# A GRU scan beside a mixture of experts: two halves of the first expert layer, and VectorE's order inside a step

## The chip, the cores and the metric

One core of one Trainium2 chip. The metric is the device time of one launch in microseconds (us), the median of several executions. Lower is better.

## What is computed

A fused model of two blocks over x of 8 batches, 256 time steps and 256 features: two recurrences with attention and expert layers, added to x in turn. The change lies in the last addition alone, a gated recurrent scan whose output feeds a mixture of eight experts and one shared expert:

```python
def step(h, xs):
    xzt, xrt, xht = xs
    z = jax.nn.sigmoid(xzt + h @ U_z + vz)
    r = jax.nn.sigmoid(xrt + h @ U_r + vr)
    hh = jnp.tanh(xht + r * h @ U + vh)
    h_new = (1.0 - z) * h + z * hh
    return (h_new, h_new)
...
gate = jnp.einsum('bsd,ed->bse', x, Wg) + routing_bias
_, top_idx = jax.lax.top_k(gate, K)
probs = jax.nn.softmax(masked_gate, axis=-1)
out = _swiglu(x, Ws1, Ws2, Ws3)
h1 = jnp.einsum('bsd,ehd->ebsh', x, W1)
h2 = jnp.einsum('bsd,ehd->ebsh', x, W2)
eo = jnp.einsum('ebsh,edh->ebsd', jax.nn.sigmoid(h1) * h1 * h2, W3)
out = out + jnp.einsum('ebsd,bse->bsd', eo, weights)
```

## The kernel before

The last stage is `pipeline_two`. It cuts the 256 time steps into 16 chunks of 16 steps (C = 16, with 8 batches a step, so CW = 128 columns a chunk). Every engine runs the same list `steps()`, pairs (i, slot): i is the chunk in the scan, slot the step in it. There is no planner: the order of calls in each engine's loop is the order of the work, and semaphores tie the loops together. A wait on an engine holds all that stands behind it on that engine.

Two kinds of work run interleaved. **The scan** of chunk i is a chain from step to step. TensorE adds U times the state for two gates (`zr_gates`, 24 small matmuls, lines L1754 and L1760; the first 16 wait for the high half of the state, the last 8 for its low half). ScalarE takes a tanh (`zr`, L1871). VectorE makes the product of gate and state in high and low halves (`reset_product`: rh_h L2030, rh L2032, rh_l L2036) and a part of the new state (zc, L2063). TensorE does the candidate (12 small matmuls, L1771 and L1776), ScalarE its tanh (`cand`, L1876), and VectorE the new state (`new_state`: zm L2042, g_hh L2047, h L2049, g_hl L2053), which the next step's `zr_gates` waits for.

**The experts** work on chunk i - 1. The hidden units of all nine experts are cut into 48 tiles, three to a group, 16 groups to a chunk, one group a slot. For group n: `hidden` on TensorE (36 matmuls of 128x128, L103: 18 for the first matrix of the layer into bank p1, 18 for the second into p2), `half_tanh` on ScalarE (th, L1895) from p1, and one slot later `swiglu` on VectorE (uu L1942 from th and p1, then a L1951 from uu and p2), `high` on ScalarE (a_h, L1886) and the low half on GpSimd (a_l, L1928). Two slots later comes `down` on TensorE (9 matmuls of 128x256, L1812). In nine of the 16 slots (0, 2, 4, 6, 7, 9, 11, 12 and 14) an expert is complete and `add_expert` adds it on VectorE (acc, L1967).

Some slots hold more, under `misc`: slot 0 reads the routing logits (lg, L1976) and, in `swiglu`, multiplies by the experts' weights (uw, L1947); slots 1 and 2 do the routing on VectorE (max, subtraction L1981, index, cast L1985; then L1988, L1991, L1994 and three more up to wts, L2000); slot 2 adds the input products of half a chunk on TensorE; slot 3 writes the output; slot 6 takes in the next chunk on VectorE (hs L1679, gx_h L2014, gx_l L2016); slot 8 splits the routing weights (wt_h on ScalarE L1914, wt_l on VectorE L2020); slot 12 adds the input products of the other half.

The order of one step on each engine is, before the change:

```python
# TensorE: zr_gates, misc, hidden, candidate, down
# ScalarE: reset_gates, high, candidate, half_tanh
# VectorE: swiglu, add_expert, reset_product, zc, misc, new_state
```

Of the kernel before, what the change touches and what calls it, by code (L numbers as in the profile page):

```python
# [26 lines left out]
ALU = mybir.AluOpType  # L27
# [9 lines left out]
CW = C * B  # L37
# [1414 lines left out]
GM = 3  # L1452
# [23 lines left out]
def pipeline_two(nc, t, arena, attd, x2d, m12_h, m12_l, out):  # L1476

    with ExitStack() as ctx:
# [3 lines left out]
        def sem(name):  # L1482
            return ctx.enter_context(nc.semaphore(name))
# [94 lines left out]
        def tile(name, dt=F16):  # L1578
# [34 lines left out]
        zr_pe, zr_act, u_pe, u_act = (sem(n) for n in ("zr_pe", "zr_act", "u_pe", "u_act"))  # L1613
        rh_hi, rh_32, rh_lo, z_parts, z_mix, h_new, h_hi, h_lo = (
            sem(n) for n in ("rh_hi", "rh_32", "rh_lo", "z_parts", "z_mix", "h_new", "h_hi3", "h_lo3"))
        hid_pe, th_act, u_done, uw_done, a_done, a_hi, a_lo, w3_pe, po_free = (
            sem(n) for n in ("hid_pe", "th_act", "u_done", "uw_done", "a_done", "a_hi3", "a_lo3", "w3_pe", "po_free"))
        z_full, z_free = sem("z_full3"), sem("z_free3")
        route, exp_done, wt_hi, wb_done = (sem(n) for n in ("route3", "exp3", "wt_hi3", "wb_done"))
        x3_done, x3_split, out_done = (sem(n) for n in ("x3_done", "x3_split", "out_done"))  # L1620
# [119 lines left out]
        def _(pe):  # L1740
# [36 lines left out]
                                         start=False, stop=(k == KT - 1), skip_group_check=True)  # L1777
                last.then_inc(u_pe, 1)

            def hidden(i, slot):  # L1780
                n = group(i, slot, 0)
                if n is None:
                    return
                par = (i - 1) % 2
                if slot == 0:
                    pe.wait_ge(h_lo, i * C)
                if n >= 2:
                    pe.wait_ge(a_done, n - 1)
                for mat, bank in enumerate((p1[n % 2], p2[n % 2])):
                    for j in range(GM):  # L1790
                        w = (lambda k: m12_h[:, mat, k, GM * slot + j, :], lambda k: m12_l[:, mat, k, GM * slot + j, :])
                        last = split_matmul(pe, bank[:, j * CW:(j + 1) * CW], w,
                                            (lambda k: g_hh[:, par, k, :], lambda k: g_hl[:, par, k, :]), j == 0,
                                            last=True)
                last.then_inc(hid_pe, 1)

            def down(i, slot):
                n = group(i, slot, 2)
# [48 lines left out]
            for i, slot in steps():  # L1847
                if scans(i):
                    zr_gates(i, slot)
                    if slot == 2:  # L1850
                        if i > 0:
                            pe.wait_ge(u_act, i * C)
                        project_half(pe, 1)
                    if slot == 12 and scans(i + 1):
                        pe.wait_ge(x3_split, 2 * (i + 1))
                        pe.wait_ge(u_act, i * C + 8)
                        project_half(pe, 0)
                misc(i, slot)
                hidden(i, slot)
                if scans(i):  # L1860
                    candidate(i, slot)
                if (i, slot) == (1, 2):
                    pe.wait_ge(m3_lo, NG)
                down(i, slot)


        @block.scalar
        def _(act):
            def reset_gates(i, slot):
                act.wait_ge(zr_pe, i * C + slot + 1)  # L1870
                act.activation(zr[:, :], g_b[slot // 8][:, slot % 8, 0:4].rearrange("p m b -> p (m b)"), ACT.Tanh,  # L1871
                               scale=0.5 / S).then_inc(zr_act, 1)

            def candidate(i, slot):
                act.wait_ge(u_pe, i * C + slot + 1)
                act.activation(cand[:, :], g_b[slot // 8][:, slot % 8, 4:6].rearrange("p m b -> p (m b)"), ACT.Tanh,  # L1876
                               scale=1.0 / S).then_inc(u_act, 1)

            def high(i, slot):
                n = group(i, slot, 1)  # L1880
                if n is None:
                    return
                act.wait_ge(a_done, n + 1)
                if n >= 2:
                    act.wait_ge(w3_pe, n - 1)
                act.activation(a_h[:, n % 2, :], a32[:, n % 2, :], ACT.Copy).then_inc(a_hi, 1)  # L1886

            def half_tanh(i, slot):
                n = group(i, slot, 0)
                if n is None:  # L1890
                    return
                act.wait_ge(hid_pe, n + 1)
                if n >= 2:
                    act.wait_ge(u_done, n - 1)
                act.activation(th[:, n % 2, :], p1[n % 2][:, 0:GM * CW], ACT.Tanh, scale=0.5 / S).then_inc(th_act, 1)  # L1895

            act.activation(cand[:, 0:1], wts[:, 0:1], ACT.Exp)
            for i, slot in steps():
                if scans(i):
                    reset_gates(i, slot)  # L1900
                high(i, slot)
                if i == 0:
                    act.wait_ge(m3_staged[slot % 4], 16 * (slot // 4 + 1))
                    staged, hi, _lo = piece(slot)
                    act.activation(hi, staged, ACT.Copy, scale=S).then_inc(m3_hi, 1)  # L1905
                if scans(i):
                    candidate(i, slot)
                half_tanh(i, slot)
                if slot == 1 and 1 <= i <= NCH:
                    act.wait_ge(route, NR * (i - 1) + 2)  # L1910
                    act.activation(rt[:, 1, :], rt[:, 0, :], ACT.Exp).then_inc(exp_done, 1)
                if slot == 8 and 1 <= i <= NCH:
                    act.wait_ge(z_full, Z3_AT[i, slot] + 1)
                    act.activation(wt_h[:, :], z[0:EA, 0:P], ACT.Copy, scale=S).then_inc(wt_hi, 1)  # L1914
                if slot == 10 and 1 <= i <= NCH:
                    act.wait_ge(z_full, Z3_AT[i, slot] + 1)
                    if i > 1:
                        act.wait_ge(uw_done, i - 1)
                    act.activation(wb[:, :], z[:, 0:GM * CW], ACT.Copy).then_inc(z_free, 1)
# [13 lines left out]
        def _(dve):  # L1933
            def swiglu(i, slot):
                n = group(i, slot, 1)
                if n is None:
                    return
                weighted = n % NG == REM
                dve.wait_ge(th_act, n + 1)
                if n >= 1:  # L1940
                    dve.wait_ge(a_done, n)
                dve.scalar_tensor_tensor(out=uu[:, :], in0=th[:, n % 2, :], scalar=1.0,  # L1942
                                         in1=p1[n % 2][:, 0:GM * CW], op0=ALU.add, op1=ALU.mult).then_inc(u_done, 1)
                dve.wait_ge(u_done, n + 1)
                if weighted:
                    dve.wait_ge(z_free, Z3_AT[n // NG + 1, 10] + 1)
                    dve.tensor_tensor(uw[:, :], uu[:, :], wb[:, :], ALU.mult).then_inc(uw_done, 1)  # L1947
                    dve.wait_ge(uw_done, n // NG + 1)
                if n >= 2:
                    dve.wait_ge(a_lo, n - 1)  # L1950
                dve.scalar_tensor_tensor(out=a32[:, n % 2, :], in0=(uw if weighted else uu)[:, :], scalar=0.5 / S / S,  # L1951
                                         in1=p2[n % 2][:, 0:GM * CW], op0=ALU.mult, op1=ALU.mult).then_inc(a_done, 1)

# [99 lines left out]
                dve.tensor_tensor(hl, h32[:, :].rearrange(kb, b=B), hh, ALU.subtract).then_inc(h_lo, 1)  # L2053

            for i, slot in steps():
                swiglu(i, slot)
                add_expert(i, slot)
                if scans(i):
                    reset_product(i, slot)
                if slot == 0:  # L2060
                    misc(i, slot)
                if scans(i):
                    dve.scalar_tensor_tensor(out=zc[:, :], in0=zr[:, 0:16], scalar=1.0, in1=h32[:, :],  # L2063
                                             op0=ALU.subtract, op1=ALU.mult).then_inc(z_parts, 1)
                if slot != 0:
                    misc(i, slot)
                if i == 0:
                    dve.wait_ge(m3_hi, slot + 1)
                    staged, hi, lo = piece(slot)
                    dve.scalar_tensor_tensor(out=lo, in0=staged, scalar=S, in1=hi, op0=ALU.mult,  # L2070
                                             op1=ALU.subtract).then_inc(m3_lo, 1)
                if scans(i):
                    new_state(i, slot)
# [86 lines left out]
```

## Time and profile before

| | us |
|---|---|
| median of 3 runs | 2818.0 |
| lowest and highest run | 2813.54 and 2818.51 |
| the profiled execution's own time | 2814.62 |
| its span | 2812.6 |
| TensorE busy, matmuls | 2424.7 |
| TensorE busy, weight loads | 2022.1 |
| VectorE busy | 1965.6 |
| ScalarE busy | 1144.6 |
| GpSimd busy | 431.1 |
| mean granted TensorE clock, share of full speed | 0.94 |

The page lists for each engine what it was busy with and what ended its idle time. The changed stage begins near 1680 us of the span and ends with it; its scan of chunks 1 to 15 runs from 1729 to 2688 us. Matmuls are pipelined, and an idle TensorE shows better in the start times of the weight loads than in the busy share of the matmuls.

### The profile page before, as it was taken

The page shows a single profiled execution, that of the slowest core. Times are in us where ns is not written, and L with a number is a line of the kernel's source. Part 1 is how long each engine was busy: PE and PEld are TensorE (multiplying, and loading weights), DVE is VectorE, ACT ScalarE, POOL GpSimd, SP SyncE. Part 2 cuts the span into 40 slices and gives each one's busy share as a digit, 9 for nine tenths or more (in the row PEclk, how much of TensorE's full clock was granted, in tenths as well). Part 3 has the DMA queues.
Part 4 walks back from the last instruction along what each step waited for, and adds up shares of the span by engine and source line. Part 5 has one row for each costly group of instructions (what it writes and reads, how often), then busy time and mean ns, then how long its engine had stood idle before and what let it go on. Part 6 is the DMA issues. An engine that isn't in the chain of part 4 may idle for free. (4 is left out here: it accounts for less than half of the span.)

```text
span 2812.6 us, 119114 instructions
## 1 busy us (share of the span) xinstructions
PE 2424.7 (86%) x50764; PEld 2022.1 (72%) x50764; DVE 1965.6 (70%) x7376; ACT 1144.6 (41%) x3659; POOL 431.1 (15%) x404
## 2 busy tenths in 40 slices
PE   1678999999999999987547846999999999999999
PEld 0455677777777777654216636999999999999998
DVE  4567777777777777787578736777766777777775
ACT  3124555555555555566126623333333333333333
POOL 0000000000000000000029910222222222222222
PEclk9778999999999999999669967999999999999999
DMA  5000000000000000000013332000000000000000
GB/s 166 2 2 2 5 5 5 5 5 5 5 5 5 5 5 5 5 5 4 3 69 87 88 90 57 9 9 9 11 9 9 9 9 9 9 9 9 5 5 6
DMA packets 52745, 53.77 MB, mean 19 GB/s; under 512 B 24678, under 2 KB 46839, under 8 KB 50041
## 3 DMA queue, kind: packets, MB, share of 16 engines
q1 hardware_dynamic: 47284, 27.79, 3.6%
q0 software_dynamic: 2000, 14.68, 1.5%
q8 instruction: 402, 6.59, 1.0%
q10 hardware_dynamic: 2934, 3.69, 0.4%
q14 instruction: 125, 1.02, 0.1%
HBM read 39.59 MB, written 6.55 MB: 16 GB/s over the span
## 5 line engine op out<-in xcount | busy, mean ns | idle before, releaser
L103 PE MATMUL p<-g_hl,m_h 128*128 128x128 f16 x3072 | 528.7, 219 | 0.0
L103 PE MATMUL p<-g_hh,m_h 128*128 128x128 f16 x3072 | 528.7, 219 | 0.0
L103 PE MATMUL p<-g_hh,m_l 128*128 128x128 f16 x3072 | 528.6, 219 | 0.0
L765 DVE STREAM_TRANSPOSE gt<-lg_b 128x512 f32<-128x512 f32 x324 | 230.3, 711 | 216.5 <-PE lg_b L448 202.6
L1928 POOL TENSOR_TENSOR a_l<-a,a_h 128x384 f16<-128x384 f32 x256 | 233.9, 914 | 915.9 <-ACT a_h L1886 915.9
L642 ACT ACTIVATE gl<-gt 128x128 f32<-128x128 f32 x324 | 100.2, 309 | 629.2 <-DVE gt L765 629.1
L657 ACT ACTIVATE hm<-xy,b 128x512 f32<-128x512 f32 x512 | 347.4, 678 | 0.1
L103 PEld LDWEIGHTS p<-g_hh,m_h 128*128 128x128 f16 x3072 | 300.4, 98 | 1.8
L103 PEld LDWEIGHTS p<-g_hh,m_l 128*128 128x128 f16 x3072 | 300.6, 98 | 0.7
L103 PEld LDWEIGHTS p<-g_hl,m_h 128*128 128x128 f16 x3072 | 300.7, 98 | 0.0
L448 PE MATMUL lg_b<-a_wh_hi,lh 128*32 128x256 f16 x4096 | 217.4, 291 | 79.0 <-DVE lh L789 76.8
L448 PE MATMUL lg_b<-e_wh_hi,lh 128*32 128x256 f16 x4096 | 209.6, 282 | 47.5 <-DVE lh L789 46.8
L448 PEld LDWEIGHTS lg_b<-a_wh_hi,lh 128*32 128x32 f16 x4096 | 100.6, 100 | 161.7 <-DVE lh L789 130.4
L1812 PE MATMUL po<-m_h,a_h 128*128 128x256 f16 x768 | 208.5, 271 | 1.9 <-DVE acc L1967 1.9
L1812 PE MATMUL po<-m_h,a_l 128*128 128x256 f16 x768 | 209.0, 272 | 0.0
L1812 PE MATMUL po<-m_l,a_h 128*128 128x256 f16 x768 | 208.8, 272 | 0.0
L1876 ACT ACTIVATE cand<-g_b 128x16 f32<-128x16 f32 x256 | 46.9, 183 | 382.8 <-PE g_b L1776 382.8
L614 PE MATMUL yo<-hm,w2f 128*32 128x256 f32 x2048 | 161.5, 388 | 34.8 <-DVE tmp L815 34.7
L2042 DVE SCALAR_TENSOR_TENSOR zm<-zr,cand 128x16 f32<-128x16 f32 x256 | 44.3, 173 | 201.2 <-ACT cand L1876 200.3
L1886 ACT ACTIVATE a_h<-a 128x384 f16<-128x384 f32 x256 | 133.9, 523 | 106.1 <-DVE a L1951 106.1
L1754 PEld LDWEIGHTS g_b<-g_hh,gu_w 128*128 128x128 f16 x4096 | 136.5, 96 | 50.9 <-DVE g_hh L2047 45.8
L1754 PE MATMUL g_b<-g_hh,gu_w 128*128 128x8 f16 x4096 | 140.5, 166 | 35.9 <-DVE g_hh L2047 34.8
(421 smaller groups left out, 6900.7 us busy)
## 6 DMA issues: line engine op xcount, KB each, us to landing
m_stage<-in_m_w POOLq DMA_DIRECT2D x12, 1024.0 KB, 5.3
hs<-in_m_w SPq DMA_DIRECT2D x16, 384.0 KB, 3.2
xs<-in_x POOLq DMA_DIRECT2D x1, 2048.0 KB, 8.4
x_dram<-x SPq DMA_DIRECT2D x16, 128.0 KB, 2.2
s_v<-in_l_wv SPq DMA_DIRECT2D x1, 2048.0 KB
attention_dram<-att SPq DMA_DIRECT2D x16, 128.0 KB, 2.7
attr<-attention_dram SPq DMA_DIRECT2D x128, 16.0 KB, 1.7
x2r<-x_dram SPq DMA_DIRECT2D x16, 128.0 KB, 2.5
```

The source lines that it names most:

```text
L103: ins = pe.matmul(out, w[wp](k), x[xp](k), start=start, stop=last and k == KT - 1 and xp == 1, skip_group_check=True)
L448: last = pe.matmul(gate_block(ae, j, par), lh[:, part, ae, k, u, :], columns(w[name], k, j), start=False, stop=(part == 1 and k == KT - 1) ...
L614: last = pe.matmul(yo[q * HD:(q + 1) * HD, :, :], w2f[:, n % E1, :], tok[:, :, q, :], start=True, stop=True, skip_group_check=True, tile_p ...
L642: act.activation(gl[:, :].rearrange("p (m b) -> p m b", b=B), gt[:, :].rearrange("p (m n) -> p m n", n=32)[:, :, slot % QS * B:(slot % QS ...
L657: act.activation(hm32[:, n % 2, h * 512:(h + 1) * 512], xy[h][:, :], ACT.Gelu, bias=b1[:, n % E1:n % E1 + 1], scale=1.0 / S).then_inc(g_32, 1)
L765: dve.transpose(gt[:, :], lg_b[slot // QS % 2][:, :, :, :].rearrange("p g a x -> p (g a x)"))\
L1754: pe.matmul(o[:, slot % 8, m, :], w[:, k, m * P:(m + 1) * P], h(g_hh, k), start=False, stop=False, skip_group_check=True)
L1812: last = pe.matmul(po[:, half, :], x[:, n % 2, r], w[:, tl, :], start=(first and x is a_h and w is m3_h), stop=(end and x is a_l), skip_gr ...
L1876: act.activation(cand[:, :], g_b[slot // 8][:, slot % 8, 4:6].rearrange("p m b -> p (m b)"), ACT.Tanh, scale=1.0 / S).then_inc(u_act, 1)
L1886: act.activation(a_h[:, n % 2, :], a32[:, n % 2, :], ACT.Copy).then_inc(a_hi, 1)
L1928: pool.tensor_tensor(a_l[:, n % 2, :], a32[:, n % 2, :], a_h[:, n % 2, :], ALU.subtract).then_inc(a_lo, 1)
L2042: dve.scalar_tensor_tensor(out=zm[:, :], in0=zr[:, 0:16], scalar=1.0, in1=cand[:, :], op0=ALU.add, op1=ALU.mult).then_inc(z_mix, 1)
```

## The change

The order in each step is now:

```python
# TensorE: zr_gates, misc, hidden (first matrix), candidate, hidden (second matrix), down
# ScalarE: reset_gates, half_tanh, candidate, high
# VectorE: reset_product, zc, misc of slot 0, swiglu, add_expert, misc, new_state
```

The first matrix's end is told by `hid_pe` as before, the second's by a new semaphore `gate_pe`, for which VectorE's last product `a` now waits as well. No operation is added or taken away.

```diff
-            def hidden(i, slot):
+            def hidden(i, slot, mat):
                 n = group(i, slot, 0)
...
-                if slot == 0:
+                if slot == 0 and mat == 0:
                     pe.wait_ge(h_lo, i * C)
-                if n >= 2:
+                if n >= 2 and mat == 0:
                     pe.wait_ge(a_done, n - 1)
-                for mat, bank in enumerate((p1[n % 2], p2[n % 2])):
-                    for j in range(GM):
...
+                bank = (p1, p2)[mat][n % 2]
+                for j in range(GM):
...
+                last.then_inc((hid_pe, gate_pe)[mat], 1)
...
                 misc(i, slot)
-                hidden(i, slot)
+                hidden(i, slot, 0)
                 if scans(i):
                     candidate(i, slot)
+                hidden(i, slot, 1)
...
-                high(i, slot)
+                half_tanh(i, slot)
                 if i == 0:
...
                 if scans(i):
                     candidate(i, slot)
-                half_tanh(i, slot)
+                high(i, slot)
...
                 if n >= 2:
                     dve.wait_ge(a_lo, n - 1)
+                dve.wait_ge(gate_pe, n + 1)
...
             for i, slot in steps():
+                if scans(i):
+                    reset_product(i, slot)
+                    dve.scalar_tensor_tensor(out=zc[:, :], in0=zr[:, 0:16], scalar=1.0, in1=h32[:, :],
+                                             op0=ALU.subtract, op1=ALU.mult).then_inc(z_parts, 1)
+                if slot == 0:
+                    misc(i, slot)
                 swiglu(i, slot)
                 add_expert(i, slot)
-                if scans(i):
-                    reset_product(i, slot)
-                if slot == 0:
-                    misc(i, slot)
-                if scans(i):
-                    dve.scalar_tensor_tensor(out=zc[:, :], in0=zr[:, 0:16], scalar=1.0, in1=h32[:, :],
-                                             op0=ALU.subtract, op1=ALU.mult).then_inc(z_parts, 1)
                 if slot != 0:
                     misc(i, slot)
```

Here is VectorE's order at slot 6 of a middle chunk, the slot that takes in the next chunk, before the change (line, operation, written tile, read tiles, shape, semaphores waited for):

```order
L1942 SCALAR_TENSOR_TENSOR uu<-th,p 128x384 [waits a_done,th_act]
L1951 SCALAR_TENSOR_TENSOR a<-uu,p 128x384 [waits a_lo3,u_done]
L1967 SCALAR_TENSOR_TENSOR acc<-po,wts,acc 128x256 [waits po_free,w3_pe]
L2030 SCALAR_TENSOR_TENSOR rh_h<-zr,h 128x16 [waits h_new,zr_act]
L2032 SCALAR_TENSOR_TENSOR rh<-zr,h 128x16
L2036 TENSOR_TENSOR rh_l<-rh,rh_h 128x16 [waits rh_32,rh_hi]
L2063 SCALAR_TENSOR_TENSOR zc<-zr,h 128x16
L1679 TENSOR_TENSOR hs<-z,x2r 128x2x128 [waits z_full3]
L2014 TENSOR_SCALAR gx_h<-hs 128x256 [waits x3_done]
L2016 TENSOR_TENSOR gx_l<-hs,gx_h 128x256 [waits x3_split]
L2042 SCALAR_TENSOR_TENSOR zm<-zr,cand 128x16 [waits u_act]
```

And the same slot in the changed kernel, whose line numbers are a little other:

```order
L2032 SCALAR_TENSOR_TENSOR rh_h<-zr,h 128x16 [waits h_new,zr_act]
L2034 SCALAR_TENSOR_TENSOR rh<-zr,h 128x16
L2038 TENSOR_TENSOR rh_l<-rh,rh_h 128x16 [waits rh_32,rh_hi]
L2060 SCALAR_TENSOR_TENSOR zc<-zr,h 128x16
L1943 SCALAR_TENSOR_TENSOR uu<-th,p 128x384 [waits a_done,th_act]
L1953 SCALAR_TENSOR_TENSOR a<-uu,p 128x384 [waits gate_pe,a_lo3,u_done]
L1969 SCALAR_TENSOR_TENSOR acc<-po,wts,acc 128x256 [waits po_free,w3_pe]
L1679 TENSOR_TENSOR hs<-z,x2r 128x2x128 [waits z_full3]
L2016 TENSOR_SCALAR gx_h<-hs 128x256 [waits x3_done]
L2018 TENSOR_TENSOR gx_l<-hs,gx_h 128x256 [waits x3_split]
L2044 SCALAR_TENSOR_TENSOR zm<-zr,cand 128x16 [waits u_act]
```

The three expert products have moved from ahead of the scan's product to between it and the new state, and hs, gx_h and gx_l now stand straight behind them.

ScalarE's order at slot 8, where the routing weights are split, before:

```order
L1871 ACTIVATE zr<-g_b 128x32 [waits zr_pe]
L1886 ACTIVATE a_h<-a 128x384 [waits w3_pe,a_done]
L1876 ACTIVATE cand<-g_b 128x16 [waits u_pe]
L1895 ACTIVATE th<-p 128x384 [waits u_done,hid_pe]
L1914 ACTIVATE wt_h<-z 9x128 [waits z_full3]
```

and in the changed kernel:

```order
L1872 ACTIVATE zr<-g_b 128x32 [waits zr_pe]
L1896 ACTIVATE th<-p 128x384 [waits u_done,hid_pe]
L1877 ACTIVATE cand<-g_b 128x16 [waits u_pe]
L1887 ACTIVATE a_h<-a 128x384 [waits w3_pe,a_done]
L1915 ACTIVATE wt_h<-z 9x128 [waits z_full3]
```

th and a_h have changed places around cand, and wt_h stands behind a_h instead of th.

## Rows read from the trace of the kernel before

**Rows 1.** Slots 0, 2, 5, 8, 9: length, busy PE, PEld, DVE, ACT, POOL, clock, DMA.

```profile
2003.20:2007.76 4.56, 4.40 (x91) 4.16 (x88) 3.93 (x13) 1.29 (x4) 0.91 (x1) 1.00 0.01 4
2011.66:2016.95 5.29, 5.29 (x132) 5.18 (x129) 4.22 (x17) 1.28 (x4) 0.91 (x1) 1.00 0.01 3
2025.07:2028.96 3.89, 3.89 (x84) 3.79 (x82) 2.08 (x10) 1.29 (x4) 0.91 (x1) 1.00 0.00 0
2037.45:2042.19 4.74, 4.28 (x85) 3.89 (x82) 2.23 (x11) 1.42 (x5) 0.91 (x1) 1.00 0.11 31
2042.19:2046.20 4.01, 3.95 (x80) 3.77 (x81) 3.25 (x12) 1.28 (x4) 0.91 (x1) 1.00 0.01 4
```

**Rows 2.** Timeline, two waits of the weight loads in chunk 5 (start us, us, engine).

```profile
2006.77 0.17 PEld L1776 LDWEIGHTS g_b<-rh_l,gu_w 128*128 128x128 f16 x4 [0.25 <-DVE rh_l L2036]
...
2033.22 0.18 DVE L2047 SCALAR_TENSOR_TENSOR g_hh<-zc,zm 128x16 f16<-128x16 f32 x1
...
2033.45 0.47 PEld L1754 LDWEIGHTS g_b<-g_hh,gu_w 128*128 128x128 f16 x16 [0.35 <-DVE g_hh L2047]
```

**Rows 3.** Timeline, weight loads of slot 5 of chunk 5.

```profile
2025.55 0.27 PEld L1760 LDWEIGHTS g_b<-g_hl,gu_w 128*128 128x128 f16 x8
2025.75 0.10 PEld L103 LDWEIGHTS p<-g_hh,m_h 128*128 128x128 f16 x1
...
2027.73 0.31 PEld L1771 LDWEIGHTS g_b<-rh_h,gu_w 128*128 128x128 f16 x8
```

**Rows 4.** Timeline, ScalarE, VectorE and GpSimd, end of slot 5 and slot 6.

```profile
2028.26 0.18 ACT L1876 ACTIVATE cand<-g_b 128x16 f32<-128x16 f32 x1 [1.30 <-PE g_b L1776]
...
2028.48 0.17 DVE L2042 SCALAR_TENSOR_TENSOR zm<-zr,cand 128x16 f32<-128x16 f32 x1 [1.53 <-ACT cand L1876]
2028.69 0.17 DVE L2047 SCALAR_TENSOR_TENSOR g_hh<-zc,zm 128x16 f16<-128x16 f32 x1
...
2029.06 0.17 DVE L2053 TENSOR_TENSOR g_hl<-h,g_hh 128x16 f16<-128x16 f32 x1
...
2029.75 0.55 DVE L1951 SCALAR_TENSOR_TENSOR a<-uu,p 128x384 f32<-128x384 f32 x1
...
2029.85 0.20 ACT L1871 ACTIVATE zr<-g_b 128x32 f32<-128x32 f32 x1 [1.02 <-PE g_b L1760]
...
2030.22 0.48 DVE L1967 SCALAR_TENSOR_TENSOR acc<-po,wts,acc 128x256 f32<-128x256 f32 x1
...
2030.94 0.92 POOL L1928 TENSOR_TENSOR a_l<-a,a_h 128x384 f16<-128x384 f32 x1 [2.98 <-ACT a_h L1886]
```

**Rows 5.** Timeline, VectorE beside GpSimd, attention stage and slot 4 of chunk 5.

```profile
1525.06 5.38 POOL L1211 TENSOR_SCALAR m_stage<-m_stage 128x2048 f32<-128x2048 f32 x1
1527.80 2.99 DVE L1376 TENSOR_SCALAR xn_h<-hs 128x512 f16<-128x512 f32 x1
...
2023.08 0.91 POOL L1928 TENSOR_TENSOR a_l<-a,a_h 128x384 f16<-128x384 f32 x1 [3.23 <-ACT a_h L1886]
2023.11 0.91 DVE L2036 TENSOR_TENSOR rh_l<-rh,rh_h 128x16 f16<-128x16 f32 x1
```

**Rows 6.** Groups by form, VectorE, last stage (count; busy us, mean ns).

```profile
L2016 DVE TENSOR_TENSOR gx_l<-hs,gx_h 128x256 f16<-128x256 f32 x14 | 6.0, 426 | 0.5
L1679 DVE TENSOR_TENSOR hs<-z,x2r 128x256 f32<-128x256 f32 x14 | 5.7, 410 | 0.0
...
L2014 DVE TENSOR_SCALAR gx_h<-hs 128x256 f16<-128x256 f32 x14 | 4.1, 294 | 0.5
```

**Rows 7.** Timeline, slot 8 and slot 2 of chunk 5.

```profile
2015.02 0.17 DVE L1994 TENSOR_TENSOR rt<-rt 128x8 f32<-128x8 f32 x1
...
2015.62 0.23 DVE L2000 TENSOR_SCALAR wts<-rt,sm 128x8 f32<-128x8 f32 x1
...
2041.22 0.25 ACT L1914 ACTIVATE wt_h<-z 9x128 f16<-9x128 f32 x1
...
2041.57 0.28 DVE L2020 SCALAR_TENSOR_TENSOR wt_l<-z,wt_h 9x128 f16<-9x128 f32 x1 [2.24 <-ACT wt_h L1914]
```

More of the change, by code:

```diff
@@ L1615, in pipeline_two @@
             sem(n) for n in ("rh_hi", "rh_32", "rh_lo", "z_parts", "z_mix", "h_new", "h_hi3", "h_lo3"))
-        hid_pe, th_act, u_done, uw_done, a_done, a_hi, a_lo, w3_pe, po_free = (
-            sem(n) for n in ("hid_pe", "th_act", "u_done", "uw_done", "a_done", "a_hi3", "a_lo3", "w3_pe", "po_free"))
+        hid_pe, gate_pe, th_act, u_done, uw_done, a_done, a_hi, a_lo, w3_pe, po_free = (
+            sem(n) for n in ("hid_pe", "gate_pe", "th_act", "u_done", "uw_done", "a_done", "a_hi3", "a_lo3", "w3_pe", "po_free"))
         z_full, z_free = sem("z_full3"), sem("z_free3")
@@ L1784, in hidden @@
                 par = (i - 1) % 2
-                if slot == 0:
+                if slot == 0 and mat == 0:
                     pe.wait_ge(h_lo, i * C)
-                if n >= 2:
+                if n >= 2 and mat == 0:
                     pe.wait_ge(a_done, n - 1)
-                for mat, bank in enumerate((p1[n % 2], p2[n % 2])):
-                    for j in range(GM):
[L1791 to L1795, printed above, removed]
+                bank = (p1, p2)[mat][n % 2]
+                for j in range(GM):
+                    w = (lambda k: m12_h[:, mat, k, GM * slot + j, :], lambda k: m12_l[:, mat, k, GM * slot + j, :])
+                    last = split_matmul(pe, bank[:, j * CW:(j + 1) * CW], w,
+                                        (lambda k: g_hh[:, par, k, :], lambda k: g_hl[:, par, k, :]), j == 0,
+                                        last=True)
+                last.then_inc((hid_pe, gate_pe)[mat], 1)
             def down(i, slot):
```

## Prediction

> **What bounds the kernel now.** I read the busy times by stretch first, then the timeline of single steps. From chunk 1 on TensorE is the bound: a step without extras lasts 3.89 us and TensorE is busy for all of it [rows 1]. In the times below 0 is the start of a step's first weight load. `zr_gates` takes to 0.68 (its low half starts at 0.48), the 36 matmuls of `hidden` to 2.66, so half of them is 0.99 [rows 3], and candidate and `down` fill the rest to 3.89. All other work lies beside this. TensorE loses time only where a state comes late: 0.25 us in slot 0 and 0.35 at the end of slot 6 [rows 2], most of what slot 8 is longer than a plain step (4.74 against 3.89), and 0.12 in slots 7 and 9 (4.01 [rows 1]). That is the pool from which a new order can win, some 2 us a chunk.
>
> **The change on TensorE.** Nothing is added; the candidate moves from 2.66 to 0.68 + 0.99 = 1.67. Can it be fed? ScalarE's zr tanh runs from 0.89 to 1.09 (2029.85 in a step that began at 2028.96 [rows 1, 4]). VectorE starts 0.04 after what it waits for (cand to zm [rows 4]), and the scan's product is now its first work: rh_h 1.13 to 1.30, and rh_l by the spacing of g_hh and g_hl (0.37, then 0.17 long [rows 4]) ends at 1.67. TensorE takes up a result 0.05 later (g_hh ended at 2033.40, its load began at 2033.45 [rows 2]), so 1.35 and 1.72 are possible and 1.67 and 1.90 are wanted: no wait. ScalarE's th now stands ahead of cand. th and a_h are 0.91 together (1.29 busy [rows 1] less zr's 0.20 and cand's 0.18 [rows 4]), so th ends some 0.5 after it may start at 1.9, and cand near 2.5. That costs nothing, since VectorE is busy longer, as follows.
>
> **The change on VectorE.** An operation that waits for nothing starts 0.08 ahead of the end of the one before (acc behind a [rows 4]); zc and uu follow rh_l so, and uu starts near 1.66. a ends at 2.81 (uu and a are alike, 0.55 each [rows 4], with 0.04 between). Where an expert is complete acc follows, 0.48 long [rows 4], to 3.21. The new state comes behind these. g_hh ends 0.38 after zm starts and g_hl starts 0.58 after it [rows 4]. In plain steps zm is at 2.73, g_hh ends at 3.11, and the next gates are wanted at 3.89: no wait, over 0.7 to spare. The third semaphore that a waits for I take at nothing, since acc of other steps waits for three at no visible gap; its upper end is 0.05 us.
>
> **What comes late next is the low half of the state.** In slot 4, rh_l starts 0.03 after GpSimd's a_l and then takes 0.91 us instead of 0.17, ending 0.03 behind it [rows 5]: the two do not run beside each other. a_l starts 0.64 after a's end (2030.30 to 2030.94 [rows 4]), nearly all of it a_h, and takes 0.91. In the new order that is 3.45 to 4.36. In plain steps g_hl starts at 3.31, ahead of a_l. With acc it is due at 3.71, inside a_l, so it ends at 4.39 and feeds TensorE at 4.44. The low gates are wanted at 3.89 + 0.48 = 4.37. That is 0.07 lost.
>
> The sum per chunk, by slot, as new length less old:
> - Slots 5, 10, 13, 15 (plain) and 3, 12 (extra TensorE work covers all): 0.
> - Slots 4, 11, 14 (acc): 0.07 lost now by g_hl, about as much before by rh_l in the same collision: 0. Slots 7 and 9: 3.96 against 4.01 [rows 1], -0.05 each.
> - Slot 1: max, subtraction and cast put g_hl behind a_l's start, +0.07.
> - Slot 0: lg, then uu, uw, a (0.55 each) and acc. g_hh ends near 4.30 and the gates start at 4.35 (4.31 is wanted: 4.56 [rows 1] less the 0.25 idle [rows 2]); a_l runs 4.23 to 5.14, TensorE has g_hl at 5.22 and wants it at 4.83. 4.35 + 0.39 = 4.74 against 4.56, +0.18.
> - Slot 2: L1994 reads two tiles like rh_l and is due, two short operations behind acc, at about 3.57, inside a_l; it ends at 4.39, and what follows it takes 0.66 more (2015.19 to 2015.85 [rows 7]). zm at 4.97, g_hh 0.38 later, gates at 5.40 against 5.29 [rows 1]: +0.11.
> - Slot 8: wt_h now waits for a_h, not for the candidate. a_h ends at 3.37, wt_h starts 0.10 ahead of that, 0.25 long, wt_l starts 0.10 later, 0.28 long [rows 7]: 3.90. zm 3.83, gates at 4.24 against 4.74 [rows 1]: -0.50. This is the gain of the change.
> - Slot 6: acc, hs (0.41), gx_h (0.29), gx_l (0.43) [rows 6] now stand behind the expert products and ahead of zm. hs reads PSUM and runs 3.13 to 3.54. gx_h is due at 3.57, inside a_l. What does it cost? From below its own 0.29. From above, it waits for a_l. In the attention stage the same kind of operation (a scale from f32 to f16) took 2.99 us beside a GpSimd operation that ended at 1530.44, itself ending at 1530.79 [rows 5], 0.35 after, on 512 columns where gx_h has 256; rh_l, with 16, ended 0.03 after. I take the upper end, with the middle of the two, 0.20, after a_l: gx_h ends 4.56, gx_l 5.03, zm 4.95, gates at 5.38. The slot took 2033.45 - 2028.96 = 4.49 [rows 1, 2]: +0.89.
>
> Ahead of the choice at slot 6: the rows show one blocked scale and one blocked subtraction, and they decide it. The Trainium skill (SBUF — State Buffer, the section on two separate sides) says that VectorE and GpSimd share a pair of ports under an exclusive lock, and that whichever starts first holds it for the whole instruction. By that rule gx_h, L1994 and g_hl all wait for a_l, as I have it; without the rule gx_h alone might pass. The same rule says that one SBUF input outside the two-port modes does not contend, so uu, a, acc, hs and the high halves pass, as the rows of this trace have them.
>
> Sum: 0.18 + 0.07 + 0.11 + 0.89 - 0.10 - 0.50 = +0.65 us a chunk, times 13 chunks (2 to 14) = +8.4. Chunk 1 has no uw and no acc at slots 0 and 2: +0.4. Chunk 15 has no slot 6 work: -0.2. Chunk 16 has no scan. At the very end the last group's th and uu start half a `hidden` earlier, and a, a_h, a_l, the last `down` and the output all follow it: -0.95. Total +7.6 us. Against the profiled execution (2814.62 us) that is 2822.2. The median of the runs, 2818.0, stands 3.4 above that execution; I set the forecast on the middle of the two, 2816.3, and come to 2824.
>
> **Rivals.**
> 1. gx_h passes beside a_l. Its rows of before never met a_l, and xn_h met other GpSimd operations. Then gx_h ends at 3.87, gx_l (two SBUF tiles) waits to 4.64, gates at 4.99: +0.50 at slot 6 instead of +0.89, times 14 is -5.5, total +2.1, about 2818. This is not slower by what can be measured. It decides from the point where a_l starts after gx_h's 3.57, or where a scale in two halves of width does not need GpSimd's port.
> 2. Nothing is blocked in the new order, as if a_l came second everywhere: slot 6 costs 0.20, slot 0 gains 0.21, the acc slots gain 0.08 each in three and 0.12 in two, slot 8 gains 0.50. That is near -1.0 a chunk, -15 in all, about 2801. Every row of a_l beside a two-tile subtraction speaks against it; a chain of mine that is 0.15 too late or too early would speak for it.
> 3. VectorE is later than I have it. At slot 1 the cast L1985 is due at 3.29 and a_l at 3.45. If 0.16 slips, the cast waits to 4.39 and the gates to 4.74: +0.8 in 15 chunks, +12 more. Or the third semaphore of a costs its 0.05 in nine slots: +6 more. 2830 to 2836.
> 4. The change does not do what it says: the printed order shows that it does, and I give it nothing.
>
> **How the numbers follow.** The forecast case 0.55, rival 1 0.17, rival 2 0.16, rival 3 0.12. A measurement of this kernel tells 0.2% from no change, here 5.6 us. The forecast of +7.6 is over that with 0.46 and under it with 0.09, since half its sum is slot 6. Slower: 0.46 + 0.12 = 0.58. Same: 0.09 + 0.17 = 0.26. Faster: 0.16. The range takes in rival 1 on the lowest run shown (2813) and the lower part of rival 3 (2833), and leaves out rival 2.
>
> **What would show it.** Right: plain steps at 3.89; cand running on TensorE between two blocks of 18; slot 6 near 5.4 with gx_h some 1 us long and ending behind a_l; slot 8 near 4.24; g_hl 0.7 us long in steps with acc; the wait ahead of slot 9 under 0.3. Wrong: gx_h at 0.29 beside a_l (rival 1), g_hl at 0.17 throughout (rival 2), L1985 near 1 us, or plain steps over 3.89 because the candidate waits for rh_h (rival 3 and worse).

## The result, and the profile after

| | before | after |
|---|---|---|
| median, us | 2815.77 (4 runs, 2812.98 to 2818.51) | 2864.06 (4 runs, 2857.84 to 2874.11) |
| the profiled execution's own time | 2814.62 | 2858.98 |
| its span | 2812.6 | 2857.1 |
| chunks 1 to 14 | 1728.94 to 2688.22: 959.3 | 1732.67 to 2729.89: 997.2 |
| chunk 5 | 68.44 | 71.15 |
| chunk 15, up to the start of its last step | 62.7 | 65.5 |
| from there to the end | 61.7 | 61.8 |

The changed kernel takes 1.0155 times the time before, with a 95% interval of 1.0121 to 1.0189: slower, where slower was forecast, but by 48 us and not by 7.6. The time of 2864.06 lies outside the range of 2813 to 2833. Of the 44.5 us between the two spans, 37.9 lie in chunks 1 to 14, 2.8 in chunk 15, 0.1 behind it and 3.7 ahead of chunk 1. (The stretch from 1729 to 2688 us of the kernel before, called the scan of chunks 1 to 15 above, ends where chunk 15 begins: it holds 14 chunks. The chunks are counted from 0, and the first one has no expert work.) Here are the first two rows of the page of the changed kernel (busy time, share, instructions).

```profile
span 2857.1 us, 119117 instructions
...
PE 2442.1 (85%) x50764; PEld 2020.1 (71%) x50764; DVE 1965.5 (69%) x7376; ACT 1138.2 (40%) x3659; POOL 429.9 (15%) x404
```

The work is the same: the weight loads take 2020.1 us where they took 2022.1, and VectorE is busy for 1965.5 against 1965.6. The time is idle time. The windows of chunk 5 show the steps in which it lies. First slots 0 to 3, 5, 6, 8, 9 and 11, then the whole chunk, in the columns of [rows 1].

```profile
2017.38:2022.38 5.00, 4.40 (x91) 4.11 (x89) 3.54 (x13) 1.28 (x4) 1.23 (x2) 1.00 0.01 3
2022.38:2026.80 4.42, 4.16 (x84) 3.79 (x81) 3.23 (x15) 1.38 (x5) 1.05 (x2) 1.00 0.01 4
2026.80:2032.07 5.27, 5.26 (x129) 5.11 (x130) 4.11 (x18) 1.17 (x4) 0.91 (x1) 1.00 0.01 3
2032.07:2036.43 4.36, 4.35 (x85) 3.98 (x84) 3.20 (x12) 1.29 (x4) 0.91 (x1) 1.00 0.01 3
...
2040.55:2044.44 3.89, 3.89 (x84) 3.79 (x82) 2.22 (x11) 1.28 (x4) 0.59 (x2) 1.00 0.00 0
2044.44:2049.74 5.30, 4.48 (x86) 4.05 (x84) 3.94 (x13) 1.28 (x4) 1.36 (x2) 1.00 0.04 9
...
2053.85:2058.49 4.64, 4.28 (x85) 3.89 (x83) 2.70 (x11) 1.44 (x5) 1.05 (x2) 1.00 0.01 1
2058.49:2062.60 4.11, 3.96 (x80) 3.72 (x81) 3.02 (x13) 1.28 (x4) 0.78 (x1) 1.00 0.02 4
```

```profile
2067.02:2071.23 4.21, 4.05 (x84) 3.81 (x82) 2.83 (x12) 1.28 (x4) 0.78 (x1) 1.00 0.00 0
2017.37:2088.52 71.15, 68.32 (x1412) 64.49 (x1410) 48.24 (x187) 20.85 (x67) 14.60 (x17) 1.00 0.03 8
```

The whole chunk, slot by slot:

| slot | before | forecast | after |
|---|---|---|---|
| 0 | 4.56 | 4.74 | 5.00 |
| 1 | 3.90 | 3.97 | 4.42 |
| 2 | 5.29 | 5.40 | 5.27 |
| 3 | 4.15 | 4.15 | 4.36 |
| 4 | 3.97 | 3.97 | 4.12 |
| 5 | 3.89 | 3.89 | 3.89 |
| 6 | 4.49 | 5.38 | 5.30 |
| 7 and 9, each | 4.01 | 3.96 | 4.11 |
| 8 | 4.74 | 4.24 | 4.64 |
| 11 and 14, each | 3.97 | 3.97 | 4.21 |

Slots 10, 12, 13 and 15 moved by 0.01 at most. Slot 10 lasts 4.42 in both kernels, so it is no plain step, though the forecast lists it as one; its term of 0 was right all the same. Two things are to be seen. The plain step and slots 6 and 2 came out near the forecast. And the rest splits into steps with an acc (0, 4, 7, 9, 11, 14), each 0.15 to 0.26 over the forecast, and three others, 1, 3 and 8, each 0.21 to 0.45 over it.

**The acc steps.** The chain of waits gives a first hint: it stands at 11% on VectorE and 25% on TensorE, where it stood at 7% and 30% before. The table of TensorE's waits from 1850 to 2650 us names the place (us in total, times, longest). Before, the same table held only g_hh, 5.6 us, and rh_l, 2.0 us.

```profile
PE g_b L1754 <- DVE g_hh L2049: 17.1, 35, 0.8
PE po L1812 <- DVE acc L1969: 13.5, 56, 0.6
PE po L1812 <- DVE acc L1967: 1.7, 11, 0.2
```

A new wait: `down` (L1812) for acc. In the timeline of slot 7, which begins at 2049.74:

```profile
2051.89 0.55 DVE L1953 SCALAR_TENSOR_TENSOR a<-uu,p 128x384 f32<-128x384 f32 x1
2052.36 0.48 DVE L1969 SCALAR_TENSOR_TENSOR acc<-po,wts,acc 128x256 f32<-128x256 f32 x1
2052.95 0.10 PEld L1812 LDWEIGHTS po<-m_h,a_h 128*128 128x128 f16 x1 [0.30 <-issue]
2052.98 0.27 PE L1812 MATMUL po<-m_h,a_h 128*128 128x256 f16 x1 [0.15 <-DVE acc L1969]
```

acc adds po into the sum, and `down` of the next group writes po. TensorE waits in front of it for `po_free`, that is until every expert that an earlier group completed has been added. acc follows a, ends at 3.10 of the step, and the load of `down` starts 0.11 behind that, with 0.30 us idle ahead of it. Before, VectorE did acc early, in slot 6 for one from 1.26 to 1.74 of the step [rows 4], and the table had no wait of `down`.

The wait asks for more than the buffer needs. By the code po has two halves, which the experts use in turn (`half = (n // NG * EA + e) % 2`), and in all nine acc slots `down` writes the half that acc does not read: in slot 7 acc reads expert 2 and `down` writes expert 3, whose half was free once expert 1 had been added in slot 6. `po_free` is a count, and `down` waits for it to include the expert just completed. A kernel in which this wait is one lower was not run, so what it would give is not shown.

**The other three.** Slots 3 and 8 in the timeline, and then the ranges of the two operations over the whole run (count; min, median, max ns; first and last start):

```profile
2035.43 0.91 POOL L1929 TENSOR_TENSOR a_l<-a,a_h 128x384 f16<-128x384 f32 x1 [3.45 <-ACT a_h L1887]
2035.49 0.89 DVE L2049 SCALAR_TENSOR_TENSOR g_hh<-zc,zm 128x16 f16<-128x16 f32 x1
...
2057.28 0.91 POOL L1929 TENSOR_TENSOR a_l<-a,a_h 128x384 f16<-128x384 f32 x1 [3.30 <-ACT a_h L1887]
2057.46 0.28 DVE L2022 SCALAR_TENSOR_TENSOR wt_l<-z,wt_h 9x128 f16<-9x128 f32 x1 [0.82 <-ACT wt_h L1915]
2057.67 0.55 DVE L2044 SCALAR_TENSOR_TENSOR zm<-zr,cand 128x16 f32<-128x16 f32 x1
```

```profile
L2049 DVE SCALAR_TENSOR_TENSOR g_hh<-zc,zm x256: 174/175/889, 1682.0 to 2798.3; 128x16 f16<-128x16 f32 x128
...
L2044 DVE SCALAR_TENSOR_TENSOR zm<-zr,cand x256: 161/168/556, 1681.8 to 2798.1; 128x16 f32<-128x16 f32 x128
```

g_hh and zm, 0.17 us long otherwise, are stretched until a_l is done: g_hh starts 0.06 after a_l and ends at 2036.38, 0.04 behind a_l's end at 2036.34. The forecast had taken only subtractions and the scale as held and had let "the high halves pass". Both operations read two tiles in SBUF, as the held subtractions do. In slot 8 wt_l, of whose two inputs z lies in PSUM, begins inside a_l and takes its usual 0.28.

The trace of before had a row of this kind, which the rows above lack; zc reads zr and h, both in SBUF:

```profile
2078.17 0.91 POOL L1928 TENSOR_TENSOR a_l<-a,a_h 128x384 f16<-128x384 f32 x1 [3.05 <-ACT a_h L1886]
2078.20 0.92 DVE L2063 SCALAR_TENSOR_TENSOR zc<-zr,h 128x16 f32<-128x16 f32 x1 [0.21 <-issue]
```

### The profile page after: what moved, and what is told of

Its sections match the earlier page's. It is cut to its first block and busy times, and to the rows that moved or that the text cites. A ratio compares the mean times of both kernels' runs of the same rounds, so it can differ in the third digit from the quotient of the medians.

```text
span 2857.1 us, 119117 instructions
## 1 busy us (share of the span) xinstructions
PE 2442.1 (85%) x50764; PEld 2020.1 (71%) x50764; DVE 1965.5 (69%) x7376; ACT 1138.2 (40%) x3659; POOL 429.9 (15%) x404
## 5 line engine op out<-in xcount | busy, mean ns | idle before, releaser
L103 PE MATMUL p<-g_hl,m_h 128*128 128x128 f16 x3072 | 540.9, 219 | 0.0
L103 PE MATMUL p<-g_hh,m_l 128*128 128x128 f16 x3072 | 540.6, 219 | 0.0
L103 PE MATMUL p<-g_hh,m_h 128*128 128x128 f16 x3072 | 540.4, 219 | 0.0
L1896 ACT ACTIVATE th<-p 128x384 f32<-128x384 f32 x256 | 125.6, 491 | 295.8 <-PE p L103 295.8
L1872 ACT ACTIVATE zr<-g_b 128x32 f32<-128x32 f32 x256 | 50.5, 197 | 451.8 <-PE g_b L1760 451.8
L1812 PE MATMUL po<-m_h,a_h 128*128 128x256 f16 x768 | 208.9, 272 | 22.3 <-DVE acc L1969 20.0
L2032 DVE SCALAR_TENSOR_TENSOR rh_h<-zr,h 128x16 f16<-128x16 f32 x256 | 44.9, 175 | 259.2 <-ACT zr L1872 259.2
L1812 PE MATMUL po<-m_h,a_l 128*128 128x256 f16 x768 | 209.2, 272 | 0.0
L1812 PE MATMUL po<-m_l,a_h 128*128 128x256 f16 x768 | 209.1, 272 | 0.0
```

Source lines behind the costliest of these rows:

```text
L1812: last = pe.matmul(po[:, half, :], x[:, n % 2, r], w[:, tl, :], start=(first and x is a_h and w is m3_h), stop=(end and x is a_l), skip_gr ...
L2032: dve.scalar_tensor_tensor(out=rh_h[:, :, :], in0=r3, scalar=1.0, in1=h3, op0=ALU.add, op1=ALU.mult).then_inc(rh_hi, 1)
```

## The experiments

Two theories stand at the start. One: the loss is `down` waiting for the late acc. The other: it is the new state held by a_l. To tell them apart, each is removed alone and then both. The lines of code are those of the changed kernel where nothing else is said.

**e1, acc first.** acc goes back ahead of the expert products, behind the scan's product.

```diff
-                swiglu(i, slot)
                 add_expert(i, slot)
+                swiglu(i, slot)
```

> The changed kernel with add_expert ahead of swiglu in VectorE's loop. Theory 1 (TensorE's down waits for acc's release of the output bank, 0.30 us in steps where an expert is complete): the idle time of po behind acc vanishes, slots 4, 7, 9, 11, 14 fall from 4.1 to 4.2 us to 3.9 to 4.0, slot 0 from 5.00 to about 4.4; slots 3, 6 and 8 keep 4.36, 5.30 and 4.63. A chunk about 69.1 instead of 71.15 us, some 30 us off the whole. Rival (VectorE's longer chain to the new state is what costs, acc is only part of its length): the length is the same in either order, so the slots stay within 0.05 us and the time too.

2822.06 us, ratio to the kernel before 1.0025 (1.0015 to 1.0035). Chunk 5 lasts 68.90. Here are its windows of slot 11 and of the chunk, and TensorE's whole table of waits from 1850 to 2650 us:

```profile
2052.94:2056.83 3.89, 3.89 (x83) 3.79 (x81) 2.46 (x12) 1.29 (x4) 0.07 (x1) 1.00 0.00 0
...
2004.91:2073.81 68.90, 67.30 (x1413) 64.31 (x1410) 45.13 (x187) 20.86 (x67) 14.60 (x17) 1.00 0.03 9
```

```profile
PE g_b L1754 <- DVE g_hh L2049: 19.0, 36, 0.9
PE g_b L1760 <- DVE g_hl L2055: 0.5, 2, 0.3
```

The wait for acc is gone, and the wait for g_hh is as it was (17.1 and 19.0). Slots 4, 7 and 9 are at 3.80, slots 11 and 14 at 3.89, slot 0 at 4.33. Slots 1, 3 and 8 stay at 4.36, 4.36 and 4.63. By the chunk, the edit gives back 2.25 us. It also puts a and with it a_l later (in slot 7 a_l starts at 3.73 of the step and not at 3.34), so that g_hl of the acc steps is no longer held; e3 against e2, where a_l is held back in both, gives the same for acc alone in slots 11 and 14 (4.20 and 4.21 to 3.89).

**e2, the low half held.** GpSimd begins a_l only when the step's new state is complete, so that it cannot hold up the new state of the same step.

```diff
                 if n is not None:
+                    if scans(i):
+                        pool.wait_ge(h_lo, i * C + slot + 1)
                     pool.wait_ge(a_hi, n + 1)
```

> The changed kernel with GpSimd's a_l held until the step's g_hl is done (a wait added on GpSimd, nothing else). Theory 2 (g_hh, zm, gx_h, g_hl and L1994 stand behind a_l, though g_hh and zm are three-operand operations): all of VectorE's small operations go back to 0.17 us; slot 3 from 4.36 to 4.15, slot 8 from 4.63 to about 4.25, slot 6 from 5.30 to about 4.75, slot 1 from 4.42 to about 3.95; slots 4, 11, 14 keep their 4.1 to 4.2 because of acc. A chunk about 69.4 us, 25 us off the whole. Rival (these operations are long because they wait for a semaphore, not for GpSimd): no change in their durations, and nothing gained.

2832.19 us, ratio 1.0056 (1.0036 to 1.0077). Chunk 5 lasts 69.75, 1.40 less than in the changed kernel. It is the complement of e1: slots 1, 3 and 8 fall to 3.90, 4.15 and 4.23, and slot 6 to 4.66. The acc slots stay (0 at 5.00, 11 at 4.20, 14 at 4.21), and slots 4, 7 and 9 even grow, by 0.09 to 0.13. For slots 7 and 9 the timeline shows why: the a_l that was held back meets rh_h of the next step, a product with two inputs in SBUF, and stretches it from 0.17 to 0.31; acc is 0.13 later for it. In slot 7:

```profile
2037.30 0.91 POOL L1931 TENSOR_TENSOR a_l<-a,a_h 128x384 f16<-128x384 f32 x1 [4.49 <-DVE g_hl L2057]
2037.93 0.31 DVE L2034 SCALAR_TENSOR_TENSOR rh_h<-zr,h 128x16 f16<-128x16 f32 x1 [0.71 <-ACT zr L1872]
```

The wait for acc stands, and no g_hh is held in the ranges over the whole run:

```profile
PE po L1812 <- DVE acc L1971: 17.1, 57, 0.6
```

```profile
L2051 DVE SCALAR_TENSOR_TENSOR g_hh<-zc,zm x256: 174/175/177, 1676.8 to 2770.9; 128x16 f16<-128x16 f32 x128
```

Slot 8 at 4.23 is the 4.24 of the forecast. Its chain was right, and zm's collision made the difference. Of what the hold gives back, 0.65 is slot 6, whose loss the forecast had.

**e3, both.**

> Both edits of the two runs before. If the two causes are all that was wrong, the savings nearly add: a chunk near 67.4 us, 1 us under the kernel before (68.44), so the whole is some 15 us faster than before. If a third cause is at work (the candidate between the two matrices, th ahead of cand), a chunk stays at 68.5 us or more.

2799.09 us, ratio 0.9955 (0.9934 to 0.9976), chunk 67.16. That is 3.99 us a chunk under the changed kernel, where the two edits alone give 2.25 + 1.40 = 3.65. The 0.34 of difference lie in slots 7 and 9 (0.13 each) and 6 (0.07): in slots 7 and 9 rh_h is held as in e2, but `down` no longer waits for the acc that it makes late, and both last 3.80. The two causes account for more than the whole loss of 2.71 a chunk. Without them the new order is faster than the old.

**e4, the order of TensorE and ScalarE alone.** VectorE's loop is put back as before.

```diff
             for i, slot in steps():
+                swiglu(i, slot)
+                add_expert(i, slot)
                 if scans(i):
                     reset_product(i, slot)
+                if slot == 0:
+                    misc(i, slot)
+                if scans(i):
                     dve.scalar_tensor_tensor(out=zc[:, :], in0=zr[:, 0:16], scalar=1.0, in1=h32[:, :],
                                              op0=ALU.subtract, op1=ALU.mult).then_inc(z_parts, 1)
-                if slot == 0:
-                    misc(i, slot)
-                swiglu(i, slot)
-                add_expert(i, slot)
                 if slot != 0:
```

> The changed kernel with VectorE's loop as before: only TensorE's and ScalarE's order is changed. My theory: plain slots stay at 3.89, because rh_h and rh_l of these come at 1.4 and 1.8 us; slots with acc have rh_h at 1.85 and wait about 0.3 us; down never waits for acc; a_l moves to about 3.1 to 4.0 and meets g_hl or g_hh. A chunk 69 to 71 us. The rival that blames TensorE's new order for all of the loss expects 71.15 us, the rival that blames VectorE's new order alone expects 68.4.

2808.62 us, ratio 0.9973 (0.9961 to 0.9985), chunk 68.20. From the start of chunk 15 to the end it takes 123.6 us against 124.4 before: 0.4 of that lies in chunk 15 and 0.4 behind its last step. So this half of the change is a small gain, and the loss comes when VectorE's half is added.

**e5, the order of VectorE alone,** in the kernel before. TensorE and ScalarE keep the old order.

```diff
             for i, slot in steps():
+                if scans(i):
+                    reset_product(i, slot)
+                    dve.scalar_tensor_tensor(out=zc[:, :], in0=zr[:, 0:16], scalar=1.0, in1=h32[:, :],
+                                             op0=ALU.subtract, op1=ALU.mult).then_inc(z_parts, 1)
+                if slot == 0:
+                    misc(i, slot)
                 swiglu(i, slot)
                 add_expert(i, slot)
-                if scans(i):
-                    reset_product(i, slot)
-                if slot == 0:
-                    misc(i, slot)
-                if scans(i):
-                    dve.scalar_tensor_tensor(out=zc[:, :], in0=zr[:, 0:16], scalar=1.0, in1=h32[:, :],
-                                             op0=ALU.subtract, op1=ALU.mult).then_inc(z_parts, 1)
                 if slot != 0:
                     misc(i, slot)
```

> The kernel before with VectorE's loop of the changed one; TensorE's and ScalarE's order stay. ScalarE's a_h then stands ahead of cand and waits for a (2.81), so a_l runs 3.45 to 4.36 and cand ends near 3.46. If three-operand operations with both inputs in SBUF cannot run beside a_l, zm is due inside a_l in every step, g_hh ends near 4.6 and every step with experts takes about 4.65 us: a chunk 79 to 81 us, the whole 160 to 190 us slower than before. If they could, g_hh would end at 3.9 and a plain step would last 3.95: a chunk near 69.5, with the wait of down for acc gone (TensorE reaches down at 2.99 in either case, so that part stays).

2938.64 us in one run, some 123 us slower, chunk 76.14 and the plain step 4.54. ScalarE does a_h ahead of cand here, so cand waits for the late a_h, and a_l starts before zm:

```profile
2061.69 0.91 POOL L1928 TENSOR_TENSOR a_l<-a,a_h 128x384 f16<-128x384 f32 x1 [4.74 <-ACT a_h L1886]
2061.72 0.92 DVE L2042 SCALAR_TENSOR_TENSOR zm<-zr,cand 128x16 f32<-128x16 f32 x1 [0.33 <-ACT cand L1876]
```

zm is held in 180 of the 240 steps of chunks 1 to 15, in 153 of them for over 0.8 us. The chunk was expected at 79 to 81, so the size is off by 3 to 5 us and the mechanism holds. The parts of the change don't add: one alone takes 7, the other alone costs 123, together they cost 48.

**e9, zm in PSUM.** What decides whether an operation stands behind a_l, its kind or where its inputs lie? The changed kernel, with zm written to 16 free columns of a PSUM bank. g_hh and h then read one input in SBUF and one in PSUM; nothing else moves.

```diff
+            def mix(slot):
+                return p1[(slot + 1) % 2][:, GM * CW:GM * CW + 16]
...
-                                         in1=zm[:, :].rearrange(kb, b=B), op0=ALU.mult, op1=ALU.add).then_inc(h_hi, 1)
+                                         in1=mix(slot).rearrange(kb, b=B), op0=ALU.mult, op1=ALU.add).then_inc(h_hi, 1)
```

> The changed kernel with zm written to 16 free columns of the idle p1 bank in PSUM instead of SBUF; order and waits as in the changed kernel. g_hh and h then have one input in SBUF (zc), zm itself and g_hl still two. Theory (an operation is held by a_l when both its inputs are in SBUF, whatever its kind): g_hh is 0.17 to 0.2 us long everywhere, also beside a_l; slot 3 falls from 4.36 to 4.15 us and slot 1 from 4.42 to about 4.0; slot 8, where zm is held, stays at 4.63, and slots 4, 11, 14 (acc) stay. A chunk about 70.6 instead of 71.15. Rival (any small VectorE operation that writes SBUF stands behind a_l, or g_hh waits for zm's semaphore): g_hh stays at 0.8 us and the slots as they are.

2847.73 us, ratio 1.0101 (1.0067 to 1.0135), chunk 70.57 against the changed kernel's 71.15. Slots 1 and 3 are at 3.90 and 4.15 as in e2, slot 8 at 4.64 as in the changed kernel (zm itself still reads two tiles in SBUF), slot 11 at 4.21. In slot 3, and over the whole run:

```profile
2032.26 0.91 POOL L1929 TENSOR_TENSOR a_l<-a,a_h 128x384 f16<-128x384 f32 x1 [3.44 <-ACT a_h L1887]
2032.32 0.17 DVE L2052 SCALAR_TENSOR_TENSOR g_hh<-zc,p 128x16 f16<-128x16 f32 x1
...
2032.68 0.53 DVE L2058 TENSOR_TENSOR g_hl<-h,g_hh 128x16 f16<-128x16 f32 x1
```

```profile
L2052 DVE SCALAR_TENSOR_TENSOR g_hh<-zc,p x256: 170/170/173, 1681.2 to 2788.7; 128x16 f16<-128x16 f32 x128
```

The same operation, of the same shape and at the same moment of a_l, takes 0.17 instead of 0.89, and g_hl behind it, with two inputs in SBUF, is held again. So for the three-operand product the place of the inputs decides. That does not make one input in SBUF safe for every kind: the scale gx_h, whose only input hs and whose output lie in SBUF, takes 0.94 in this run too.

**e6, the extra work behind the new state.** Can the order be had without either loss? The edit is that of e1, and beside it `misc` of slots 1 to 15 goes behind the new state, so that g_hh is done before a_l begins.

```diff
-                swiglu(i, slot)
                 add_expert(i, slot)
-                if slot != 0:
-                    misc(i, slot)
+                swiglu(i, slot)
...
                 if scans(i):
                     new_state(i, slot)
+                if slot != 0:
+                    misc(i, slot)
```

> The changed kernel with acc ahead of the expert products (as in the run with acc first) and all misc work of slots other than 0 behind the new state. Theory: what the new state waits for is now only uu and a, and it is through before a_l begins (g_hl 3.71, a_l 3.85 in steps with acc), so slot 1 falls to 3.9, slot 3 to 4.15, slot 6 from 5.37 to about 4.2, slot 8 from 4.63 to 4.0; a chunk near 66.6 us, some 25 us under the kernel before. Rival: the misc work is only put off, stands behind a_l instead (gx_h, gx_l to 5.4 us, past the next step's rh_h at 5.2) and comes back as a wait of the candidate in slots 7 and 2; then a chunk stays above 67.5.

2787.98 us, ratio 0.9898 (0.9882 to 0.9915): faster than both kernels. Its chunk, and the one line left for TensorE's weight loads in the waits from 1850 to 2650 us:

```profile
1996.07:2062.67 66.60, 66.60 (x1412) 64.70 (x1410) 43.71 (x187) 20.96 (x67) 14.60 (x17) 1.00 0.03 9
```

```profile
PEld g_b L1760 <- DVE g_hl L2055: 0.7, 2, 0.4
```

TensorE is busy for all of the 66.60 us. gx_h is still stretched by a_l (0.67), but it now stands where the new state does not wait for it. Slot 6 lasts 4.16 and slot 8 4.01, where before they lasted 4.49 and 4.74.

**e7, e6 with a_l held as in e2.**

> The same with a_l held until g_hl is done. If nothing of the state's chain meets a_l any more, holding it gains nothing: within 0.2% of the run before it. If some steps still lose to the port, 5 to 10 us faster.

2786.83 us, ratio 0.99 (0.988 to 0.9921). The two intervals cover each other: once the new state is early, the hold gains nothing that these runs can tell.

**e8, the extra work behind the new state, in the kernel before.** Is it this move that pays, and not the change?

```diff
-                if slot != 0:
-                    misc(i, slot)
...
                 if scans(i):
                     new_state(i, slot)
+                if slot != 0:
+                    misc(i, slot)
```

> The kernel before with nothing changed but the misc work of slots other than 0 put behind the new state. Of the 2 us a chunk that the old order loses, 0.35 at slot 6 and 0.74 at slot 8 are misc work ahead of the state; these go, the collision of rh_l with a_l stays: a chunk near 67.3 us, 15 us under the kernel before. If this equals the version with the new order, the new order itself gives nothing.

A miss. 2827.43 us, ratio 1.0038 (1.0017 to 1.0059), where a gain was expected. Slot 8 gains as expected (4.00), but slot 7 goes from 4.01 to 5.06 and slot 4 from 3.97 to 4.65. The weight loads of the candidate wait for the scan's product, from 1850 to 2650 us:

```profile
PEld g_b L1776 <- DVE rh_l L2036: 23.6, 46, 0.8
```

In the old order `misc` of slot 6 then stands ahead of the expert products of slot 7, and these ahead of its scan's product. In the new order the scan's product comes first in the step and only the expert products slip. So the late `misc` pays only with the change's own order of VectorE.

## Why the prediction was right and wrong

- **Bound of the kernel, plain steps at 3.89.** Right, slot 5 lasts 3.89.
- **The candidate at 1.67 is fed.** Right. In slots without wait its first load follows the 18 matmuls of `hidden`, and the waits of the changed kernel hold no line for rh_h or rh_l.
- **th ahead of cand costs nothing.** Right as far as the runs show: no wait for cand's product in the table, and with all of ScalarE's new order e6 keeps TensorE busy throughout.
- **VectorE's times in the step.** Right in plain steps and slot 6, where zm was due at 4.95 and starts at 4.87 (2049.31 less 2044.44). The third semaphore of a costs nothing: in slot 7 a begins at 2051.89, 0.03 behind uu's end at 2051.86.
- **Slot 6, +0.89.** Right, +0.81, by the mechanism named: gx_h is held by a_l. This row of the timeline has it, behind an a_l from 2047.87 to 2048.78.

```profile
2047.99 0.94 DVE L2016 TENSOR_SCALAR gx_h<-hs 128x256 f16<-128x256 f32 x1
```

  It ends at 2048.93, 0.15 behind a_l; 0.20 was taken, the middle between rows of 16 and 512 columns. Rival 1, that it passes, is out.
- **acc steps, 0 and -0.05.** This step failed. The forecast asked what acc waits for, what stands behind it and when g_hl comes, but never who waits for acc. `down` does, through po: in slot 7 its load would start at 2052.65, acc ends at 2052.84, and it starts at 2052.95. e1 takes this away and gives back 2.25 us a chunk. The collision of g_hl with a_l that the forecast had for these steps is there (0.70 long in slot 0), but the larger term was missing, not mis-sized.
- **"The high halves pass, as the rows of this trace have them".** This failed as well. No row of before had a g_hh beside an a_l, so no row could have them pass, and zc, which has the same form, was held in five rows that I did not look for. It missed +0.45 in slot 1 and +0.21 in slot 3 (g_hh), and in slot 8 +0.40 of the gain of 0.50 (zm). e2 and e9 show it. The Trainium skill (SBUF — State Buffer, the section on two separate sides) says that an instruction with one SBUF input outside the two-port modes does not contend, and speaks of two SBUF inputs as the case that does. The traces agree: 0.89 with zm in SBUF, 0.17 with zm in PSUM. The prediction read that rule as clearing the high halves, which it does not, since zc and zm both lie in SBUF.
- **Slot 2, +0.11 by L1994 held.** Measured -0.02. The reason given was wrong: a_l did not start at 3.45 there but at 4.27 (2031.07), since the extra matmuls come ahead of `hidden` and push th to 2030.02, and a_h now stands behind th. The routing operations passed ahead of it, and g_hh was held 0.83 in their place, of which the extra TensorE work covers nearly all.
- **Slot 0, +0.18.** Measured +0.44. `down` waits here too, for an acc that stands behind three long products, and e1 brings the slot to 4.33, under the 4.56 of before.
- **The tail, -0.95.** Measured +0.1, from the start of the last step to the end. The last group's th and uu did start earlier, by 0.56 (at 51.98 and 52.50 behind the start of the last step, where before it was 52.54 and 53.06). But the product uw, with two inputs in SBUF, then stood beside an a_l and took 1.20 instead of 0.56, and a ended no earlier than before (54.87 against 54.80). The forecast gave that chain no collision. In e4 uw meets a_l as well (1.19), and 0.4 of the saving is left. First the changed kernel, then the row of before:

```profile
2848.34 0.91 POOL L1929 TENSOR_TENSOR a_l<-a,a_h 128x384 f16<-128x384 f32 x1 [2.08 <-ACT a_h L1887]
2848.47 1.20 DVE L1948 TENSOR_TENSOR uw<-uu,wb 128x384 f32<-128x384 f32 x1
```

```profile
2804.53 0.56 DVE L1947 TENSOR_TENSOR uw<-uu,wb 128x384 f32<-128x384 f32 x1
```

- **The sum.** Forecast +0.65 a chunk, measured +2.71, which is 2.06 more. By the table above the acc steps are 1.19 over their forecast (0.26 in slot 0, 0.15 each in 4, 7 and 9, 0.24 each in 11 and 14), slots 1, 3 and 8 are 1.06 over (0.45, 0.21 and 0.40), and slots 2 and 6 are 0.21 under, which makes +2.04. In chunks 1 to 14 the two kernels differ by 37.9 us, where 8.8 was forecast (8.4 and 0.4 for chunk 1); 14 times 2.06 is 29 of these 29.1. Chunk 15, forecast at -0.2, was 2.8 longer, since it has the acc steps and the held zm too.
- **The direction.** Slower was forecast and slower it was, but for the greater part not for the reasons given. Slot 6 cost what was said; 2.25 us of a chunk's 2.71 come from two terms that the forecast had at nothing, `down` behind acc and the held g_hh and zm.

Rival 3 named VectorE's lateness at slot 1, and slot 1 did become late, but by g_hh and not by the cast, which ran in 0.17. Rival 2, nothing blocked and 2801, had two blocks against it. With both gone, e3 measured 2799.09.

Chunk 1 of the profiled execution after begins 3.7 us later than that of the one before. The change doesn't touch what lies ahead, and in the experiments' traces chunk 1 begins anywhere from 1724.0 us (e7) to 1745.4 us (e8). So the shift isn't put down to the change; what makes it stays open, as does why the runs of the changed kernel lie 16 us apart.

## What to carry to other kernels

When an operation is moved to a later place on its engine, list who waits for it, the semaphores by which it releases buffers above all, and set its new end against the time at which they are due; what it waits for itself is only half of the question. Ask as well whether such a wait asks for more than the buffer needs. Then go through every small operation of the critical chain and note where its inputs lie: if both are in SBUF, it must come before a long GpSimd operation like a_l, which reads SBUF too, or it is held until that is done. Moving one input to PSUM freed the three-operand product here. A scale from SBUF to SBUF was held with one input. The work that nobody waits for in this step belongs behind the chain's last operation, once the next step's first operation no longer stands behind what it delays.

## What was not expected of the hardware

- A three-operand product on VectorE (SCALAR_TENSOR_TENSOR) with two SBUF inputs is held as a TENSOR_TENSOR is: g_hh took 0.89 instead of 0.17 beside a_l, zc and zm (in e5) 0.92. With one input in PSUM it took 0.17.
- A held scale of 256 columns from f32 to f16 ended 0.15 us behind GpSimd's operation; one of 512 columns had ended 0.35 behind [rows 5], and operations of 16 columns end 0.03 to 0.04 behind. The product uw of 384 columns ended 0.42 behind.
- A third wait on a semaphore that is already satisfied shows no time: the gap ahead of a is 0.03 us in slot 7, where with two waits it was 0.03 as well.
